# A rotary attention layer with expert routing: the order of each engine written anew, on one Trainium2 core

## The reference, cut to what matters

```python
x = x + _L0_xattn_ref(_layernorm(x), ctx_1024, ctx_1024, mask, ...)
x = x + _L0_attn_ref(_layernorm(x), ...)
x = x + _L0_ffn_ref(_layernorm(x), ...)                 # 64 experts, top 8
x = x + _L1_xattn_ref(_layernorm(x), ctx_1024, ctx_1024, ...)
x = x + _L1_attn_ref(_layernorm(x), Wq, Wk, Wv, Wo)     # the rotary layer
x = x + _L1_ffn_ref(_layernorm(x), ...)                 # 8 experts, top 2

def _layernorm(x, axis=-1, eps=1e-05):
    m = jnp.mean(x, axis=axis, keepdims=True)
    v = jnp.var(x, axis=axis, keepdims=True)
    return (x - m) / jnp.sqrt(v + eps)

def _L1_attn_ref(x, Wq, Wk, Wv, Wo):                    # 16 heads of 32
    q, k = _rope(q, sin, cos), _rope(k, sin, cos)
    scores = einsum('bhqd,bhkd->bhqk', q, k) / sqrt(dk) + slopes * -abs(pos_i - pos_j)
    attn = softmax(scores)
    return einsum('bhqk,bhkd->bhqd', attn, v) @ Wo.T

def _L1_ffn_ref(x, ...):
    router_weights = softmax(x @ W_router.T + b_router)  # top 2 kept
    return einsum('bseo,bse->bso', expert_out, router_weights)
```

## Time and profile before

| | |
|---|---|
| runs of before | median 2409.91 us of 3 (2407.17 to 2411.99) |
| the profiled execution | 2414.08 us, span 2412.3 us |
| granted TensorE clock, mean of the span | 0.951 |
| PE busy | 2199.6 us (91%) |
| DVE busy | 1097.8 us (46%) |
| ACT busy | 337.3 us (14%) |
| rotary layer with routing, 2062 to 2289 us | 227 us, PE busy 179.6 us |

### The profile page before, as it was taken

One profiled execution on the slowest core, in us unless ns is written; L12 is line 12 of the kernel. 1 busy time (PEld: TensorE's weight loads), 2 busy tenths in 40 slices (PEclk: granted clock), 3 DMA queues, 4 the chain that ended last, 5 costly groups with the idle time before them and its releaser, 6 DMA issues. The chain is left out here.

```text
span 2412.3 us, 48540 instructions
## 1 busy us (share of the span) xinstructions
PE 2199.6 (91%) x19151; PEld 1648.9 (68%) x19151; DVE 1097.8 (46%) x3060; ACT 337.3 (14%) x783; POOL 245.7 (10%) x303
## 2 busy tenths in 40 slices
PE   6999899999429999999997999999999999888698
PEld 5887689898328788888884666766766766455443
DVE  3666323232563444444442554554554544465523
ACT  0000011111001111111111222212221222111010
POOL 0000000000003343333331000000000000000102
PEclk8999999999659999999998999999999999999799
DMA  7223520000606999999996212212212113400044
GB/s 249 68 70 123 174 84 1 0 0 2 236 22 222 318 327 331 329 332 330 330 308 180 84 36 100 83 35 100 83 35 100 65 52 122 183 19 19 28 127 152
DMA packets 83176, 329.09 MB, mean 136 GB/s; under 512 B 10928, under 2 KB 11568, under 8 KB 73745
## 3 DMA queue, kind: packets, MB, share of 16 engines
q1 hardware_dynamic: 63216, 277.80, 32.1%
q0 software_dynamic: 18720, 47.96, 7.6%
q10 hardware_dynamic: 1152, 2.10, 0.2%
HBM read 278.04 MB, written 51.18 MB: 136 GB/s over the span
## 5 line engine op out<-in xcount | busy, mean ns | idle before, releaser
L574 PEld LDWEIGHTS psum<-work,arena 128*128 128x128 f32 x3072 | 355.6, 193 | 31.9 <-issue 31.0
L574 PE MATMUL psum<-work,arena 128*128 128x128 f32 x3072 | 356.2, 276 | 1.4 <-ACT work L1583 1.4
L358 PEld LDWEIGHTS psum<-work,arena 128*128 128x128 f32 x2560 | 294.2, 195 | 9.3 <-issue 7.0
L358 PE MATMUL psum<-work,arena 128*128 128x128 f32 x2560 | 295.0, 278 | 3.6 <-DMA arena<-in_q 1.9
L649 PE MATMUL psum<-work,arena 128*128 128x257 f32 x1024 | 233.8, 382 | 0.8 <-DVE arena L1289 0.8
L364 PE MATMUL psum<-arena,work 128*128 128x512 f32 x448 | 212.7, 629 | 20.9 <-DVE small L907 11.9
L672 PE MATMUL psum<-work 128*128 128x512 f32 x512 | 225.7, 594 | 6.0 <-ACT work L1498 5.2
L1498 ACT COPY work<-psum 128x512 f32<-128x512 f32 (+1 forms) x214 | 112.9, 553 | 812.6 <-PE psum L295 706.3
L1716 POOL TENSOR_TENSOR small<-small 128x1 f32<-128x1 f32 x136 | 77.7, 571 | 1415.2 <-issue 901.6
L649 PEld LDWEIGHTS psum<-work,arena 128*128 128x128 f32 x1024 | 190.6, 191 | 28.0 <-issue 1.2
L582 PE MATMUL psum<-arena,work 128*128 128x512 f32 x384 | 182.0, 610 | 2.0 <-DVE work L1240 2.0
(11 more groups left out here) (227 smaller groups left out, 2208.4 us busy)
## 6 DMA issues: line engine op xcount, KB each, us to landing
arena<-in_experts SPq DMA_DIRECT2D x64, 2304.0 KB, 10.1
expert_rows<-work SPq DMA_DIRECT2D x8, 2304.0 KB, 9.4
work<-in_ctxT SPq DMA_DIRECT2D x32, 514.0 KB, 4.3
work<-in_ctx SPq DMA_DIRECT2D x32, 512.0 KB, 3.9
work<-in_ctx_tail SPq DMA_DIRECT2D x32, 450.0 KB, 3.4
arena<-in_experts SPq DMA_DIRECT2D x8, 1024.0 KB, 17.2
arena<-in_qkv SPq DMA_DIRECT2D x1, 6144.0 KB, 19.1
work<-expert_rows SPq DMA_DIRECT2D x21, 256.0 KB, 2.7
```

The source lines that it names most:

```text
L358: done = nc.tensor.matmul(to[:, n * P:(n + 1) * P], w[:, j, at:at + P], src[:, j * P:(j + 1) * P], start=(j == 0), stop=(j == KD - 1))
L574: done = nc.tensor.matmul(to[:, n * P:(n + 1) * P], w[:, at:at + P], xgT[e % 2][:, j * P:(j + 1) * P], start=(j == 0), stop=(j == KD - 1))
```

## The change

For the rotary layer each of the three engines gets a stream of its own, `rotary()`, in place of the shared one:

- PE: `queries_keys` (i+1), `values` (i), value projection, `project_out` (i), `rest_keys`, then positions of tile i-2, turning of rows of tile i-1, turning of tile i+2, scores (i+1), logits of tile i-1. A tile's logits come at the end of one pass, its choice and positions in the next.
- DVE: the softmax function is split into `shift_scores` and `turn_probs`. One `step_(i)` shifts the scores, takes the logits of tile i-2, turns the probabilities, rotates queries and keys, normalises the rows of tile i-1, chooses the experts of tile i-2, adds the output, normalises tile i+2, takes the places of tile i-2. Its loop has 4 rounds where there were 5.
- ACT: it copies the product of probabilities and values out of PSUM (`take_out`), which DVE did, and exponentiates the logits right after the scores.
- `inverse_root` replaces `inverse_roots` wherever there is one column: one operation for the first guess and two `scalar_tensor_tensor` for each of three rounds, 7 in all. The form for 7 columns in the first expert layer stays.
- A memset of wmat is dropped.

The diff, without what only leaves the shared functions:

```diff
+SHARES = [-0.5 ** (13 / 27), 0.5 ** (4 / 9), -0.5 ** (1 / 3)]
+SEED = float(0x5F3759DF) - 13 / 27 * 2.0 ** 23 - 2.0 ** 31
...
+            def rotary():
+                turn_xn()
+                queries_keys(True)
+                taken = c.proj.value()
+                project("v", True)
+                turned = rest_keys(taken)
+                turn_xn()
+                scores(turned)
+                pe.wait_ge(s_w[st.loads["out"]], 16)
+                for i in range(TILES - 1):
+                    queries_keys()
+                    taken = c.proj.value()
+                    values()
+                    project("v")
+                    project_out()
+                    turned = rest_keys(taken)
+                    if i >= 2:
+                        positions_in_experts(pe, c)
+                    if i == 1:
+                        pe.wait_ge(s_w["tables1"], 16 * TABLES1)
+                    if i >= 1:
+                        rows = turn_rows(pe, c, i - 1)
+                    if i + 2 < TILES:
+                        turn_xn()
+                    scores(turned)
+                    if i >= 1:
+                        choice_logits(pe, c, rows)
+                rows = turn_rows(pe, c, TILES - 2)
+                values()
+                positions_in_experts(pe, c)
+                choice_logits(pe, c, rows)
+                project_out()
+                positions_in_experts(pe, c)
+
+            if st.rope:
+                rotary()
+                return
...
+        def inverse_root(dve, var, root, step):
+
+            nc.vector.tensor_scalar(root.bitcast(I32), var.bitcast(I32), -0.5, SEED, ALU.mult, ALU.add)
+            for share in SHARES:
+                dve.drain()
+                nc.vector.scalar_tensor_tensor(step, root, var, root, ALU.mult, ALU.mult)
+                dve.drain()
+                nc.vector.scalar_tensor_tensor(root, step, 3.0 * share * share, root, ALU.subtract, ALU.mult)
+            dve.drain()
...
-            inverse_roots(dve, var, half, root, step)
+            inverse_root(dve, var, root, step)
...
+            def shift_scores(i=None):
...
-                between()
+
+            def turn_probs(i=None):
...
+            def softmax(i, between=lambda: None, after=lambda: None):
+                shift_scores(i)
+                between()
+                turn_probs(i)
...
+            def rotary():
                 dve.wait_ge(s_w["rope"], 16)
                 dve.wait_ge(s_w["alibi"], 16)
+                first()
+                layernorm_measured(dve, 1)
+                nc.vector.memset(cumb1, 0.0)
+                nc.vector.memset(upto0, 0.0)
+                nc.vector.memset(upto1, 0.0)
+
+                def step_(i, places=True, rows=True, ahead=True):
+                    shift_scores()
+                    if places:
+                        take_choice_logits(dve, c)
+                    turn_probs()
+                    first()
+                    if rows:
+                        normalise_rows(dve, i - 1)
+                    if places:
+                        choose_experts(dve, c, i - 2)
+                    for half_ in range(2):
+                        add_to_x(i, half_)
+                    if ahead:
+                        layernorm_measured(dve, i + 2)
+                    if places:
+                        take_places(dve, c, i - 2)
+                step_(0, False, False)
+                dve.wait_ge(s_w["tables1"], 16 * TABLES1)
+                step_(1, False)
+                with rounds(dve, TILES - 4, [(c.proj, st.per_proj), (c.s, st.rows), (c.e, 1), (c.route, 1)]) as i:
+                    step_(i + 2)
+                step_(TILES - 2, ahead=False)
+                shift_scores()
+                take_choice_logits(dve, c)
+                normalise_rows(dve, TILES - 2)
+                turn_probs()
+                choose_experts(dve, c, TILES - 3)
+                take_places(dve, c, TILES - 3)
+                take_choice_logits(dve, c)
+                choose_experts(dve, c, TILES - 2)
+                for half_ in range(2):
+                    add_to_x(TILES - 1, half_)
+                take_places(dve, c, TILES - 2)
+                normalise_rows(dve, TILES - 1)
+
...
+            def rotary():
+                own = [a.rearrange("p b (k n) -> p b k n", n=S) for a in (
+                    psum[:, SCORE * BANK:(SCORE + SEQS) * BANK].rearrange("p (b n) -> p b n", b=SEQS)[:, :, 0:st.chunks * S],)][0]
+
+                def take_out():
+                    c.vals.add(st.rows)
+                    wait(act, s_o, c.vals.value())
+                    nc.scalar.copy(oT[:, 0:D].rearrange("p (k b n) -> p b k n", b=SEQS, n=S), own).then_inc(s_o_ready, 1)
+
+                def step_(places=True, rows=True, ahead=True):
+                    exps()
+                    if places:
+                        choice_exp()
+                    take_out()
+                    for to in (v, qT, kT):
+                        act_take(act, c, to[:, 0:D])
+                    if rows:
+                        take_rows()
+                    if ahead:
+                        take_xn()
+                c.vals.add(TILES * (xattn0.rows + attn0.rows))
+                take_xn()
+                for to in (v, qT, kT):
+                    act_take(act, c, to[:, 0:D])
+                take_xn()
+                step_(False, False)
+                step_(False)
+                with rounds(act, TILES - 4, [(c.tp, st.per_tp), (c.sm, 1), (c.route, 1), (c.vals, st.rows)]):
+                    step_()
+                step_(ahead=False)
+                exps()
+                choice_exp()
+                take_rows()
+                take_out()
+                choice_exp()
+
```

More of the change, by code:

```diff
@@ L394, in scores, with second @@
                                 done.then_inc(s_s, 1)
-            def second(first=False, turned_rows=None):
+            def second(first=False):
                 behind = c.tp.value() if st.gated else c.proj.value()
@@ L468, in rest_out, with tile @@
                 pe_project(pe, c, emit)
-            def tile(rest=False, turn=True, route=None):
+            def tile(rest=False, turn=True):
                 queries_keys()
-                if route is not None:
-                    turned_rows = turn_rows(pe, c, route)
                 values()
@@ L476, in tile @@
                     rest_values()
-                turned = second(turned_rows=None if route is None else turned_rows)
+                turned = second()
                 if rest:
@@ L500, in attention_pe @@
                 counts += [(c.ctxh, 16)]
-            if st.rope:
-                for i in range(TILES - 3):
-                    tile(route=i)
-                tile(turn=False, route=TILES - 3)
-                turned_rows = turn_rows(pe, c, TILES - 2)
-                values()
-                choice_logits(pe, c, turned_rows)
-                project_out()
-                positions_in_experts(pe, c)
-                return
             with rounds(pe, TILES - 2, counts):
@@ L1040, in take_rest_out, with tile @@
                 dve_take(dve, c, lambda src: nc.vector.tensor_copy(vrw_part, src[:, 0:P]))
-            def tile(i, ln=True, rest=False, tails=SEQS, route=None):
-                if route is not None:
-                    normalise_rows(dve, route)
+            def tile(i, ln=True, rest=False, tails=SEQS):
                 seqs = iter(range(tails if st.cross else 0))
```

84 lines of the change are left out of this document (13 added, 71 removed).

## The result

| | before | after |
|---|---|---|
| median of the runs | 2409.8 us (8: 2407.2 to 2417.7) | 2388.0 us (8: 2381.7 to 2399.8) |
| the profiled execution, its span | 2414.1, 2412.3 us | 2391.4, 2389.6 us |
| mean granted clock | 0.951 | 0.954 |
| seven passes (first to last score addition) | 166.1 us | 150.5 us |
| last score addition to first expert product | 34.9 us | 29.2 us |

The ratio is 0.9909, with a 95% interval of 0.989 to 0.9928. The forecast was 2377 with a range to 2387, so the gain came, 22 us of it, but 11 us less than forecast. The spans differ by 22.7 us: 15.6 in the passes, 5.7 in the end of the layer, 2.2 ahead of the first score addition (2087.86 against 2085.63), less 0.9 lost behind the first expert product.

The account below looks back on a forecast made before the run. PE's pass was taken as ended by DVE's late choice of experts, not PE's arithmetic. Passes -27.8, inverse root -2.3, layer end -5.9, one stall +3 sum to -33: 2414.1 to 2381 profiled, 2377 for the runs, range 2367 to 2387.

Parts of the forecast that it names:

- The waits of the old order: Rotary passes before: PE waited 0.90 and 2.59 us, then lost 1.70 to half rate, in a pass of 25.1 us.
- The rival of DVE as the bound: Rotary passes: DVE's round has waits, so a pass costs 22 us, not 20.3; 2386 us, chance 0.17.
- The seven passes, -27.8 us: Rotary layer, first to last score addition: 138.3 us instead of 166.1, with a steady pass of 20.3.
- the walk: Step-by-step count of the new order in a rotary pass: PE 20.3 us, DVE's round 18.6 us.
- Nothing in it is idle for long, so the clock stays: Rotary passes: without long idle time, PE's clock was expected to stay at 2.4 GHz, granted clock near 1.00.
- The inverse root, -2.3 us: Layer norms on DVE: seven operations take 1.97 us, not 2.74; 0.77 gained at each of three places outside the passes.
- The end of the layer, -5.9 us: Rotary layer, last score addition to first expert product: 29 us instead of 34.9, with half rate in it.
- the chain: Listed steps from last score addition to first expert product, put at 23 us at full clock.
- One stall of issue, +3 us: Rotary passes: one PE wait of issue in small products, with its half rate, taken at +3 us.
- waits of issue in more than two groups: Sign in the changed profile that would prove the stall term of +3 us wrong.
- ACT's copy: Rotary passes: ACT instead of DVE copies the values' product, about 0.7 us, and it costs nothing either way.
- The ways in which it could be slower: PE's stream runs dry in nearly every small group: 14 at 2.5 us plus lost rate, +70; 2444 us, chance 0.04.

Follow-up runs that it names:

- the late scatter: The changed kernel, with GpSimd holding each tile's scatter until the score products of the tile three further on are done: 2380.4 us, ratio 0.9854.

## Why the prediction was right or wrong

- **The waits of the old order: right.** PE no longer waits for the places, and the clock of the projections is back at 2.4 GHz in five of seven. DVE's round was put at 18.6 us and is 18.5; it waits 2.5 us for the scores (over 1 was forecast). The granted clock over the passes rose from 0.92 to 0.97, where near 1.00 was forecast. The rival of DVE as the bound is out.
- **The seven passes, -27.8 us: wrong, and this is the step that failed.** They took 150.5 us, not 138.3; the term was -15.6. The sum of full-rate work was right: with the scatter moved away, the last four passes are 20.5, 20.3, 20.5 and 19.5, where the walk had 20.3, 20.3, 20.3 and 19.7. What the walk left out is POOL. It followed every step on PE, DVE and ACT and took the scores as 1.3 us wherever they stood. But taking the places is what starts the scatter, and the change moved both places and scores so that they meet; the scores then took up to 2.00 us. Of the 12.2 us missing, the late scatter gives back 6.0 (150.5 to 144.5), 5.4 of them in the last four passes. The other 6.2 stay in that kernel too, nearly all in the second and third pass, around the stall for which the forecast had set 3 aside. In other executions the scatter perhaps cost more, since the changed kernel's runs spread over 18 us; that was not profiled.
- **"Nothing in it is idle for long, so the clock stays": wrong in one of seven.** The projection of 2214.53 took 8.81 us with no wait over 0.3 us in the 12 us ahead of it, only scores of 1.94 us. Slow small products were enough here.
- **The inverse root, -2.3 us: right for the root itself, and by luck in the sum.** From the first of the seven operations to the one behind them are 1.93 us (2182.46 to 2184.39), 1.97 forecast; the old eleven took 2.83 so measured, 2.74 forecast. That the first score addition came 2.2 us earlier is no proof of the sum. In eight executions whose program is the same up to this layer, that of the changed kernel among them, it came anywhere from 2078.5 to 2092.3, and what makes these 14 us isn't known. Taken out of the new kernel the root costs 4.8 us of the medians, and the intervals of the two ratios overlap: the first addition is 1.0 later and the end of the layer 2.3 longer.
- **The end of the layer, -5.9 us: right in size, in part by luck.** It took 29.2 us, 29 forecast, with a clock of 0.52 from 2238 to 2255. But two waits of issue, 1.2 and 2.2 us, stand in it, which the chain hadn't. And the chain's 23 can't be redone: its listed terms add up to 22.1, with no price for the output.
- **One stall of issue, +3 us: right in kind, too small.** The one in the second pass cost 2.1 us and 2.9 of half rate in the next projection, 5 us. By the prediction's own sign, waits of issue in more than two groups, the term is wrong: there are five, each in another group, two of them in the end of the layer. The rule that I quoted from the Trainium skill (Runtime: NRT & Kernel Launch, Instruction fetch mechanics), that crossing into the next block is mostly hidden, doesn't hold for these groups: PE went on 2.3 to 2.7 us after the packet of instructions. Behind the other 15 of the 20 packets in the layer no such wait follows.
- **ACT's copy: free, as said.** No engine waits for it. The test with DVE's copy was 8 us slower, far more than its 0.7 us a pass can make, and the slow scores beside the scatter are what its trace shows.

The ways in which it could be slower weighed stalls in small groups, at 2.6 us each for all 14. The size was near: up to 2.8 us a group is what the overlap costs in its bad form. But the cause was looked for in PE's own stream. Half of the loss did lie there, in the stall; the other half lay on the one engine that the walk didn't visit.

## What to carry to other kernels

When steps are moved, walk the engines that nobody waits for as well: ask what each moved step releases, and what will then run beside it. An indirect DMA that GpSimd starts belonged beside large products here, not beside a burst of small ones; a wait on GpSimd that nobody else feels, or a burst placed 2 us earlier, gained 8 and 12 us of the medians (6 and 10 in the passes). A group of small products has to be priced by what runs beside it: the same overlap cost 0.7 us in one kernel and 2.8 in another. And a forecast term is proved by its own place in the trace, not by a sum that happens to agree: over the same program, executions here differed by 14 us.

## What was not expected of the hardware

- Two indirect transfers of GpSimd, 0.98 us each, lengthen 128 small products on PE from 1.28 us to 1.94 to 2.0, or break them into runs of five or six with 0.4 to 0.5 us between (4.05 us in all). Beside 128x512 products no such break is seen (7.11 and 7.33 us with the pair beside them, 7.11 without). Which resource the two share stays open; and so does why it is mild in one kernel and bad in another, with the same 0.4 us between the starts.
- The clock fell to 1.2 GHz after a slow group with no wait over 0.3 us ahead (8.81 us at 2214.53, clock 0.61 from 2214 to 2217), and it didn't fall after two others like it (1.96 and 2.00 us, with projections of 7.11 behind them).
- A packet of instructions can stop PE within a group of small products, and PE then goes on 2.2 to 2.9 us after the packet (42 waits of issue in fourteen traces). Most packets don't stop it. Where one falls isn't set by PE's stream alone: with DVE's copy, that stream being the same, it came 1.8 us after the start of the second pass's scores, and there was no stall.
